# A three-stage transformer kernel: the gate's dot products join the first expert's matmuls, and the attention weights are brought in ahead of attention

## The reference, cut to what matters

```python
x = x + 0.5 * ffn(layernorm(x), sim_matrix, gates, q_proj, k_proj, v_proj, o_proj)
x = x + attn(layernorm(x), w_q, w_kv, w_dense)
x = x + 0.5 * ffn(layernorm(x), sim_matrix, gates, q_proj, k_proj, v_proj, o_proj)

def ffn(y, ...):                               # 16 experts, H = 128, causal attention inside
    logits = l2norm(y, -1) @ l2norm(sim_matrix, 0) - sigmoid(gates)
    w = softmax of relu(logits) over the active experts (the best two if none is active)
    q, k, v = (sum_e w[:, e] * (y @ proj[e]) for proj in (q_proj, k_proj, v_proj))
    ao = softmax(causal(q @ k.T / sqrt(H))) @ v
    return sum_e w[:, e] * (ao @ o_proj[e])

def attn(z, w_q, w_kv, w_dense):               # 16 heads of 128, 4 key/value groups
    q, k, v = z @ w_q, z @ w_kv[:, :512], z @ w_kv[:, 512:]
    return softmax(causal(q @ k.T / sqrt(128))) @ v @ w_dense
```

## Time and profile before

| | us |
|---|---|
| median of 3 runs | 2719.21 (2718.47 to 2721.8) |
| the profiled execution | 2719.64 |
| its span in the trace | 2717.8 |
| PE busy | 2598.0 (96%) |
| PEld busy | 2400.6 (88%) |
| DVE busy | 2149.8 (79%) |
| ACT busy | 944.3 (35%) |
| POOL busy | 883.6 (33%) |

### The profile page before, as it was taken

The page is one execution under the profiler, slowest core; times in us unless marked ns, Lnnn a source line. Parts: engine busy times, 40 slices in busy tenths (PEclk is TensorE's granted clock), DMA queues, the critical chain, the costliest instruction groups (busy, mean ns, idle before and its releaser), DMA issues. The chain is left out here.

```text
span 2717.8 us, 46683 instructions
## 1 busy us (share of the span) xinstructions
PE 2598.0 (96%) x14948; PEld 2400.6 (88%) x14948; DVE 2149.8 (79%) x6062; ACT 944.3 (35%) x2560; POOL 883.6 (33%) x1946
## 2 busy tenths in 40 slices
PE   5999999999994999999999999997999999999998
PEld 5999999999993889888888888896899999999997
DVE  5888888888886777787878787776888888888887
ACT  3111101101102777777777777775211011011100
POOL 3323332323221233343434343334333323232321
PEclk8999999999996999999999999998999999999999
DMA  6000000000002444455444554445200000000000
GB/s 184 4 1 1 1 1 1 1 1 1 1 1 78 78 88 88 78 89 88 88 80 91 84 88 81 85 88 116 67 1 9 9 1 9 9 9 1 9 9 9
DMA packets 378739, 117.34 MB, mean 43 GB/s; under 512 B 338560, under 2 KB 377472, under 8 KB 378496
## 3 DMA queue, kind: packets, MB, share of 16 engines
q1 hardware_dynamic: 378496, 114.36, 21.2%
HBM read 26.24 MB, written 4.19 MB: 11 GB/s over the span
## 5 line engine op out<-in xcount | busy, mean ns | idle before, releaser
L445 PE MATMUL ffn_ring<-ffn_mix_weights,ffn_yT 128*128 128x384 f32 x6144 | 1248.1, 345 | 16.0 <-DVE ffn_mix_weights L673 8.4
L445 PEld LDWEIGHTS ffn_ring<-ffn_mix_weights,ffn_yT 128*128 128x128 f32 x6144 | 1085.3, 191 | 60.5 <-issue 8.5
L612 DVE SCALAR_TENSOR_TENSOR ffn_mix_sums<-ffn_ring,ffn_w,ffn_mix_sums 128x384 f32<-128x384 f32 x896 | 550.8, 616 | 243.8 <-PE ffn_ring L445 224.7
L1486 POOL CAST attn_probsT<-attn_turned 128x1024 fp32r<-128x1024 f16 (+3 forms) x512 | 348.4, 723 | 559.6 <-DVE attn_probs L1350 556.1
L496 PE MATMUL ffn_ring<-ffn_out_weights,ffn_avT 128*128 128x512 f32 x1536 | 441.1, 398 | 2.8 <-POOL ffn_avT L904 2.8
L1422 ACT ACTIVATE attn_exponentials<-attn_exponentials,attn_score_neg_max 128x512 f32<-128x512 f32 (+3 forms) x512 | 285.0, 558 | 163.0 <-DVE attn_score_neg_max L1333 162.9
L496 PEld LDWEIGHTS ffn_ring<-ffn_out_weights,ffn_avT 128*128 128x128 f32 x1536 | 284.0, 189 | 29.0 <-POOL ffn_avT L904 4.3
L1198 PE MATMUL attn_scores<-attn_kT,attn_qT 128*128 128x256 f32 (+2 forms) x1536 | 295.9, 326 | 11.2 <-DVE attn_score_neg_max L1333 7.9
L1198 PEld LDWEIGHTS attn_scores<-attn_kT,attn_qT 128*128 128x128 f32 x1536 | 244.0, 188 | 45.9 <-DVE attn_score_neg_max L1333 13.8
L1198 PE MATMUL attn_ctx<-attn_probsT,attn_v 128*128 128x256 f32 (+2 forms) x1536 | 272.1, 326 | 0.3 <-POOL attn_probsT L1486 0.2
L1350 DVE SCALAR_TENSOR_TENSOR attn_probs<-attn_exponentials,attn_prob_factor,attn_probs 128x512 f16<-128x512 f32 (+3 forms) x512 | 248.4, 546 | 18.3 <-ACT attn_probs L1431 18.1
(11 more groups left out here) (135 smaller groups left out, 2589.9 us busy)
## 6 DMA issues: line engine op xcount, KB each, us to landing
ffn_mix_stage<-in_L_ffn_q_proj_dram SPq DMA_DIRECT2D x32, 128.0 KB, 2.6
ffn_mix_stage<-in_L_ffn_k_proj_dram SPq DMA_DIRECT2D x32, 128.0 KB, 2.6
ffn_mix_stage<-in_L_ffn_v_proj_dram SPq DMA_DIRECT2D x32, 128.0 KB, 2.9
ffn_out_stage<-in_L_ffn_o_proj_dram SPq DMA_DIRECT2D x16, 256.0 KB, 3.3
attn_turned<-attn_probs SPq DMA_TRANSPOSE x256, 4.0
out_dram<-x SPq DMA_DIRECT2D x8, 512.0 KB, 3.0
x<-in_L_attn_x_dram SPq DMA_DIRECT2D x7, 512.0 KB, 7.9
attn_weight_stage<-in_L_attn_w_q_dram SPq DMA_DIRECT2D x4, 512.0 KB, 8.3
```

The costliest lines, as they stand in the source:

```text
L445: last = pe.matmul(bank[:, 0:QKV], yT[:, t % 2, h, k * P:(k + 1) * P], wm[:, e, wh, k], start=(n == 0), stop=(n == 3 * CK - 1))
L612: dve.scalar_tensor_tensor(into, bank[:, 0:QKV], w[:, t, e:e + 1], into, ALU.mult, ALU.add).then_inc(mix_done, 1)
L1486: pool.tensor_copy(cast(i), landed(n, i).rearrange("p (j h q) -> p j h q", h=HL, q=P)).then_inc(t_cast, 1)
```

## The change

There are two parts.

**Gate columns.** `sim_weights` is copied once per FFN (ScalarE) behind expert 0's `hi` weights, which become 416 columns wide (`WIDE`). `mix(T, 0)` and `gate_dots(T)` become one `mix_first(T)`: six matmuls, four of 416 and two of 384 columns, in a fifth bank `head` of its own. It stands where `gate_dots` stood, so expert 0 of tile T + 1 is multiplied in slot T at e = 2. VectorE reads the dots and the sum of expert 0 from `head`.

**Attention weights.** The block between `ffn1` and `attention` goes. k and v pieces are loaded into the FFN's own staging memory as soon as its output weights are split, q pieces into the memory of experts 0 to 2 once the last tile is past them (`last_tile_past`); ScalarE splits them from slot 31 on, VectorE in slot 32. The four dense pieces are loaded at the start of attention and split in the first two of its slots; the fourth load waits for `aw.lo` of 9. GpSimd's clearing of `probsT`, whose memory they pass through, moves behind these.

The hunks stand in this order: SP in `ffn`, TensorE in `ffn` (three), VectorE and ScalarE (two) in `ffn`, and SP, VectorE and ScalarE in `attention`.

```diff
+EARLY_LO = (5, 6, 8, 9, 12, 13, 14, 15)
...
+EARLY = 8
+LATE = 4
...
+    def split_hi(self, act, n, dst=None, stage=None):
+        raw, hi, _ = self.parts(n, dst, stage)
+        self.wait_loaded(act, n)
+        act.activation(hi, raw, ACT.Copy).then_inc(self.hi, 1)
+
+    def split_lo(self, dve, n, dst=None, stage=None):
+        raw, hi, lo = self.parts(n, dst, stage)
+        dve.wait_ge(self.hi, n + 1)
+        dve.tensor_tensor(lo, raw, as_f32(hi), ALU.subtract).then_inc(self.lo, 1)
...
+        def last_tile_past(eng, size):
+
+            eng.wait_ge(mix_ready, (E - 1) * (TILES - 1) + -(-size // (8 * CK * QKV)) - 1)
...
@@ -377,6 +469,16 @@
             for g in range(STAGE_OUT, OG):
                 load_out(g)
+            if aw:
+                for n in range(EARLY):
+                    if n == 0:
+                        for g in range(OG - STAGE_OUT, OG):
+                            split_done(sp, E + g)
+                    if n == LATE:
+                        last_tile_past(sp, 4 * LATE * Q_COLS)
+                    src, _, _, _, width = aw.pieces[n]
+                    raw = aw.parts(n)[0]
+                    sp.dma_start(raw, src).then_inc(aw.loaded[n % EARLY], 16)
...
@@ -389,7 +491,7 @@
-                p = i - RING
+                p = i - RING if i != RING or not inside(T, 0) else -RING
...
@@ -416,25 +518,26 @@
-            def gate_dots(T, t):
-
+            def mix_first(T, t):
...
-                reach(pe, dot_read, T)
+                reach(pe, mix_done, E * (T - 1) + 1)
+                n = 0
                 for k in range(CK):
-                    for half in range(2):
-                        last = pe.matmul(sc[:, 0:2 * E], yT[:, t % 2, half, k * P:(k + 1) * P], m.simw[:, k],
-                                         start=(k == 0 and half == 0), stop=(k == CK - 1 and half == 1))
-                last.then_inc(dots_ready, 1)
+                    for h, wh in ((0, 0), (0, 1), (1, 0)):
+                        moving = mix_half(0, 1)[:, k] if wh else gate_columns(slice(0, WIDE))[:, k]
+                        width = QKV if wh else WIDE
+                        last = pe.matmul(head[:, 0:width], yT[:, t % 2, h, k * P:(k + 1) * P], moving,
+                                         start=(n == 0), stop=(n == 3 * CK - 1))
+                        n += 1
+                last.then_inc(head_ready, 1)
...
@@ -498,16 +600,14 @@
             def slot(T, t):
                 for e in range(E):
-                    if inside(T, 0):
+                    if inside(T, 0) and e > 0:
                         mix(T, t, e)
-                    if isinstance(T, int) and T == 0 and e == 0:
-                        gate_dots(0, 0)
...
                     if e == 2 and inside(T, -1):
-                        gate_dots(T + 1, (t + 1) % QT)
+                        mix_first(T + 1, (t + 1) % QT)
...
@@ -721,6 +825,8 @@
+                    if aw and T == TILES and e in EARLY_LO:
+                        aw.split_lo(dve, EARLY_LO.index(e))
...
@@ -814,6 +920,10 @@
+                    if aw and T == TILES - 1 and e >= E - LATE:
+                        early_split_hi(act, e - (E - LATE))
+                    if aw and T == TILES and e < EARLY - LATE:
+                        early_split_hi(act, LATE + e)
...
@@ -821,6 +931,8 @@
                 const.split_hi(act)
+                act.wait_ge(const.lo, 1)
+            act.activation(gate_columns(slice(QKV, WIDE)), as_f32(m.simw[:]), ACT.Copy).then_inc(sim_in, 1)
             split_weights(0)
...
@@ -1176,19 +1237,17 @@
         @block.sync
         def _(sp):
+            for n in range(EARLY, EARLY + LATE):
+                if n == EARLY + LATE - 1:
+                    sp.wait_ge(aw.lo, EARLY + 1)
+                sp.dma_start(aw.parts(n, wd, stage)[0].rearrange("p (h c) -> p h c", c=C),
+                             aw.pieces[n][0]).then_inc(aw.loaded[n % EARLY], 16)
...
@@ -1397,6 +1458,9 @@
                 place("F")
+                if b == 0 and h < 2:
+                    for n in (EARLY + 2 * h, EARLY + 2 * h + 1):
+                        aw.split_lo(dve, n, wd, stage)
...
@@ -1461,6 +1525,9 @@
                 place("F")
+                if b == 0 and h < 2:
+                    for n in (EARLY + 2 * h, EARLY + 2 * h + 1):
+                        aw.split_hi(act, n, wd, stage)
```

172 lines of the change are left out of this document (91 added, 81 removed).

## The result

The changed kernel takes 2688.9 us (median of 4 runs, 2686.15 to 2692.05), where the kernel before takes 2720.5 beside it (4 runs). The ratio is 0.9884, 95% interval 0.9871 to 0.9897: 31.6 us less. The forecast was 2693, with a range from 2681 to 2703. The profiled execution took 2686.15 us (span 2684.4), 33.5 less than the profiled one before.

The account below looks back on a forecast made before the run. TensorE's stream was taken to bound the steady FFN, while TensorE idled in the block before attention. Steady tiles -11.6, ends -0.4, block -21.4, drain +1.0, attention +6.0 sum to -26.4 us from 2719.21: 2693, range 2681 to 2703.

Parts of the forecast that it names:

- The block: Between ffn1 and attention: loading and splitting the attention weights, with TensorE idle, goes; -21.4 us.
- Rival E: Attention's start: loads wait for memory freed late, the 21.4 us come back as waits; about 2708, chance 0.04.
- The stream saving: Steady FFN tiles: four dots and a dearer group leave TensorE's stream, 32 columns in four matmuls come; net 0.38 us a tile.
- The wait: Steady FFN slots: TensorE just misses VectorE's sum of expert 0 before `mix(T, 2)`; costs 0.18 us a tile.
- Rival A: FFN slot's wait costs nothing: weight load not held, or VectorE a little earlier; 10.4 us more gain, 2682, chance 0.20.
- The ends of the FFNs: First and last slots of ffn1 and ffn2: small gains and losses around the steady tiles, together -0.4 us.
- The drain: ffn1's end: VectorE's splits behind `av` delay slot 33's first sum by 2.0 us, part recovered; +1.0 us.
- That takes back 1.0: ffn1's slot 33: eight pairs of sums at VectorE's own pace, about 0.88 us instead of 1.01, recover 1.0 us.
- Attention: Attention's first two slot changes: splits of dense pieces delay the loop through `split_probs`, 3.0 us each; +6.0 us.

Follow-up runs that it names:

- e6_w_earlier: The changed kernel with the gate weights made before the last projection's sums instead of behind them; 2687.35 us.
- e3_sum_later: The changed kernel with VectorE's layer norm statistics put ahead of the sum of expert 0 in every steady slot; 2701.49 us.
- e2_gate_only: The kernel before with the gate columns alone, the block between ffn1 and attention still there; 2704.16 us, ratio 0.9937.

## Why the prediction was right, and where it was not

**The block.** -21.4 forecast, -21.34 measured, and nothing came back as a wait for loads. Rival E is out.

**The stream saving.** 0.38 a tile forecast; with the wait removed (`e6_w_earlier`) a tile is 24.80 - 24.39 = 0.41 shorter. The 90 ns a dot of the trace held; with 25 ns the gain would have been some 15 us less. The Trainium skill (TensorE: Matmul & The Clock Gate, Back-to-back issue gap) gives the 25 ns for a matmul by itself and says of these figures that at few columns they count too little, because the weight load is not in them; each dot had one, so the prediction set a figure for another case against the row.

**The wait.** This is the step that failed: 0.18 a tile was forecast, about 0.065 is paid (58 x 0.115 = 6.7 us too pessimistic). The price of a missed wait was right: 0.06 and 0.12 forecast; in `e3_sum_later`, where the sum ends 0.09 behind the request, TensorE starts 400.73 - (400.08 + 0.60) = 0.05 behind the sum, and the weight load costs 0.13. What was wrong is the sentence that the sum "hangs on the last projection and the gate weights, not on where expert 0's matmuls stand". Before, the sum was released by `mix(T, 0)`, 0.10 later than `w` alone would have released it, and with expert 0 out of the slot it ends 1.88 behind the slot's start and not 1.98. Rival A, "VectorE is a little earlier", with a chance of 0.20, is for the most part what happened. The forecast said that 0.1 us decides, and then took a side.

**The ends of the FFNs.** Forecast -0.4, measured in this pair about -4, and most of the difference is not firm. In ffn1, slot 2 begins 1.96 earlier (80.44 to 78.48) against 1.05 forecast; in the other runs with gate columns and attention weights it begins at 77.9 to 79.7, in `e2_gate_only` at 80.57. Slots 30 and 31 together gain nothing (from slot 30's transposes to the transposes of q and k in slot 32, 50.39 before, 50.34 after); that was forecast, as -0.2 and +0.2. ffn2 gains 12.3: 10.0 in the 28 slots from 2 to 29, 0.8 ahead of them and 1.5 behind them. The 1.5 is the granted clock: from slot 30's transposes to the sum over `av` TensorE had 0.97 of the full clock before and 1.00 after (63.06 and 61.52 us), and over all traces this stretch takes 61.5 us where the clock was 1.00 and 62.0 to 63.1 where it was 0.96 or 0.97. The clock parts the runs in ffn2's slot 1 too: it was 1.00 before and in both traces of the changed kernel, and 0.93 with the gate columns alone and the attention weights alone, where ffn2 begins its slot 2 at 62.1 and 63.5 us behind its first transposes instead of 60.3 and 59.5. No run shows why it was granted so.

**The drain.** +1.0 forecast, +2.24 measured. The first sum of slot 33 was to be 2.0 later and is 1.71 later, measured from `av`. "That takes back 1.0" failed, and could not have held: it needs eight pairs of sums at 0.88 us each, but wherever VectorE doesn't wait for a bank a pair takes 0.98, in slot 33 of every trace. Before, five of the seven distances were 0.98 already; only the other two (1.28 and 1.05) had anything to give, 0.37 in all. TensorE, late through GpSimd and at half clock, then held the first pairs of the changed kernel instead. Neither GpSimd's work on `av` nor the clock had a term in the sum.

**Attention.** +6.0 forecast for the splits, +5.73 measured, by the mechanism named. Not in the forecast: 1.02 in unit 2 and 4.68 in the units behind it. The 1.02 and 3.4 of the 4.68 are program fetches that fall on transposing DMAs; the remaining 1.3 is open.

**The sum.** Against the traces' 33.5 the forecast of 26.4 is 7.1 too small. It was too pessimistic by 6.7 in the wait, 1.7 in the stream saving (58 x 0.03) and 3.7 at the FFNs' ends, and too optimistic by 1.2 in the drain and 3.7 in attention (5.7 in units 2 to 126, less 0.3 in the splits, 0.6 in the prologue and 1.1 behind the last unit). That these cancel in part is luck: the forecast is closer than its terms.

## What to carry to other kernels

When a step moves, ask for each consumer which of its releasers was the last, and by how much the second was earlier: a wait that "hangs on A" may hang on B 0.1 us later, and where a wait is met to the hundredth, either answer can be right. The distance between the end of each candidate and the start of the waiting instruction, over many slots, tells them apart: 0.14 was too long for a sum that waits for `w`. If VectorE gets work with two SBUF inputs, look up what GpSimd does beside it and who waits for that; and when an edit removes two suspects at once, look among the other traces for one that has only one of them. And before a small gain or loss is put down to an edit, run the same edit's code size alone: 36 empty instructions took 3 us off this kernel.

## What the hardware showed that was not expected

- Beside VectorE's subtractions of 128x1024 with both inputs in SBUF, GpSimd's 128x128 cast took 1.15 us instead of 0.29, its subtraction 1.31 instead of 0.46, and its 128x256 addition 1.71 instead of 0.73; VectorE's pair took 3.01 instead of 2.44.
- A 16 KB fetch of TensorE's program among a transposing DMA's packets makes it land after 5.2 us instead of 4.0. In two traces of the same program it falls on the same units, and it moved when 36 instructions were added or some 290 taken out ahead.
- With the granted clock at 0.57 instead of 1.00, two groups of six 512-column matmuls took 2.29 and 2.32 us instead of 1.44 and 1.56. The same drain of ffn1 took 12.86 us where the clock over the projections' first 4 us was 0.50, and 11.73 where it was 1.00.
- VectorE's pair of sums (128x256, one input in PSUM) comes every 0.98 us when nothing holds it, though each of the two is 0.48 long; where TensorE at 1.2 GHz holds it, every 1.28.
